# Outer tap columns of the offset sums moved by four transfers; the ninth sampling piece of a strip with 48 columns

## The chip, the core and the metric

One core of a Trainium2 chip runs the whole program in one launch. The metric is the device time in microseconds. TensorE (PE) multiplies, VectorE (DVE), ScalarE (ACT) and GpSimd (POOL) work element by element, SyncE (SP) issues transfers; ScalarE's queue can issue transfers as well.

## What is computed

Two metaformer layers on x of shape (4, 128, 128, 128). The change touches the first block alone, a deformable 3x3 convolution on the normalised input:

```python
def _L0_conv_ref(x, w_off, w_conv):              # x is _ln_c(x)
    offset = conv3x3(x, w_off, padding=1)        # 18 channels: (dy, dx) of 9 taps
    dy, dx = offset.reshape(B, 9, 2, H, W)[:, :, 0], ...[:, :, 1]
    py, px = base_y + dy, base_x + dx
    sampled = bilinear_gather(x, py, px)         # zero outside the image
    return einsum("bckhw,ock->bohw", sampled, w_conv)
x = x + _L0_conv_ref(_ln_c(x), w_off, w_conv)
```

A mixture of experts, a convolution by Fourier transform and a second mixture of experts follow. They are the same in both kernels.

## The kernel before

The first stage (`phase_a`) works in strips of four image rows; 4 images of 32 strips make 128 (the last of an image has six centre rows). `order_a` writes one list of steps for all engines: strip s has its time slots t0 to t0 + 11 (18 for the last of an image), `put(slot, step, ...)` puts a step into a slot, and each engine goes through the list and does the steps that are its own, in that order. Several strips are in the pipeline at once: in slot group s the letters are F = s + 4 (load, transpose, statistics, norm), Z = s + 2 (offset sums), N = s + 1 (weights of the samples), s itself (sampling), and s - 2 (output).

For one strip, in the order of the data:

- `turn` (L350, PE): four transposes of the input into a bank; `stats` (L496, L499, DVE): mean and variance; `scale` (L562 to L568, POOL): their power; `norm` (L437, ACT); `norm_out` (L446, ACT's queue): the normalised strip goes to DRAM (`xtp`).
- `conv` (L361, PE): 162 columns for each of four rows: the 18 offset channels for three tap rows and three tap columns, not yet summed; `y_out` (L464, ACT): scaled copies into the ring `a_yr`.
- `zsum` (L589, L595, POOL): the sum over the tap rows, into `zz`, with image x on the partitions. What is missing is the sum over the three tap columns kx, where kx = 0 and 2 belong to the neighbouring partition.
- `shift` (L374, PE): two matmuls with a shifted unit matrix do that move for kx = 0 and kx = 2, into a PSUM area `OF` (72 columns); `offs` (L517, DVE) adds kx = 1 and writes `on`, the offsets; `offs_out` (L450, ACT's queue) stores them.
- `place` (L623) and `hats` (L607, L610), POOL: distance of each offset from eight positions in x and in y; `bend` (L473, ACT) and `clip` (L528, DVE); `reach` (L522, L523, DVE): largest and smallest offset.
- `prod` (L536 on DVE, L576 on POOL): the products, 9 taps of 64 weights for each image row; `turn_s` (L545, DVE): their transposes into `tt`.
- `window` (L658, SP): 16 transfers of 36 KB from `xtp` to `win` for each strip. They wait for the store of the normalised strip. `x1_out` (L676) and `load` (L643) are 256 KB each on the same queue.
- `sample` (L405, PE): nine pieces of 36 positions in x of both halves, in three thirds h = 0, 1, 2. Each matmul uses 32 rows of the array, four stand side by side; fp32 makes two halves (instructions) of each, so 144 in all. Thirds 0 and 2 use banks 0 to 3, third 1 banks 4 to 7, where `turn` and `conv` write too. `evict` (L482 on ACT, L509 on DVE) copies each third into `a_sr`.
- `out` (L423, PE): nine matmuls with 512 columns, one for each tap; `residual` (L551, DVE) adds the input.

TensorE waits in this stage at the first third (transposed weights, windows), at the second third for `norm`, `stats`, `y_out` and `residual`, and at the third third for the emptying of the first.

## Time and profile before

| | us |
|---|---|
| median of three runs | 3873.46 (3870.35 to 3874.3) |
| the profiled execution | 3877.71 |
| its span, first to last instruction | 3875.7 |
| TensorE busy | 3679.2 |
| VectorE busy | 2944.7 |
| ScalarE busy | 1570.9 |
| GpSimd busy | 1474.4 |
| mean granted clock of TensorE | 0.956 |

The profile is of one execution. Its times are us from the first instruction, and a line Lnnn is one of the kernel before. A busy share is an average over stages; the stage of the change is the first half of the span. A row of the timeline merges neighbours of one line: start, length, engine, line, what it writes and reads, and how many instructions; brackets tell the idle time of the engine before it and who ended it.

### The profile page before, as it was taken

What the parts mean: (1) busy time and instruction counts of PE and PEld (TensorE: products, weight loads), DVE (VectorE), ACT (ScalarE), POOL (GpSimd) and SP (SyncE); (2) the same over time, 40 slices, a digit from 0 to 9 for tenths busy, and PEclk for the clock granted to TensorE, in tenths of its full rate; (3) what the DMA queues carried; (4) which work ended last, traced back from release to release, by engine and by line L of the source; (5) the groups of instructions that cost most, each with busy time, mean ns of one, the idle gap of its engine ahead of it and who ended that gap; (6) DMA issues with size and microseconds to landing.
All of it is one profiled execution on the core that took longest, in us unless ns stands there. A gap on an engine that the chain in (4) does not pass through costs nothing. (4 is left out here: it accounts for less than half of the span.)

```text
span 3875.7 us, 89814 instructions
## 1 busy us (share of the span) xinstructions
PE 3679.2 (95%) x31511; PEld 2470.7 (64%) x31511; DVE 2944.7 (76%) x9687; ACT 1570.9 (41%) x4565; POOL 1474.4 (38%) x2661
## 2 busy tenths in 40 slices
PE   6999999999999999999979999999999999996667
PEld 5777777777777777777745666666666666654444
DVE  4666666666666666666648999999999999996633
ACT  3444444444444444444411444434343443434224
POOL 4444444444454444444412333333333333333210
PEclk7999999999999999999979999999999999997755
DMA  5655555555555555555527777777777777884789
GB/s 109 108 95 108 100 95 97 96 108 104 91 99 95 108 103 94 96 97 97 88 81 265 270 275 274 272 268 273 277 271 275 267 276 273 285 303 158 268 312 393
DMA packets 611250, 709.81 MB, mean 183 GB/s; under 512 B 62208, under 2 KB 493824, under 8 KB 594416
## 3 DMA queue, kind: packets, MB, share of 16 engines
q1 hardware_dynamic: 505328, 630.10, 58.3%
q10 hardware_dynamic: 104448, 71.85, 6.0%
q8 instruction: 253, 4.15, 0.5%
q14 instruction: 197, 1.61, 0.2%
q0 software_dynamic: 1024, 2.10, 0.2%
HBM read 521.26 MB, written 181.50 MB: 181 GB/s over the span
## 5 line engine op out<-in xcount | busy, mean ns | idle before, releaser
L423 PE MATMUL a_sb<-a_sr,wcv 128*128 128x512 f32 (+3 forms) x2820 | 1052.2, 515 | 0.8 <-DVE a_xo L551 0.8
L405 PEld LDWEIGHTS a_sb<-a_tt,a_win 32*128 32x128 f32 x19008 | 647.0, 186 | 116.3 <-issue 115.5
L423 PEld LDWEIGHTS a_sb<-a_sr,wcv 128*128 128x128 f32 x2820 | 493.1, 190 | 333.9 <-issue 289.1
L405 PE MATMUL a_sb<-a_tt,a_win 32*128 32x144 f32 x19008 | 679.8, 295 | 17.5 <-ACT a_yr L464 11.0
L1171 DVE TENSOR_TENSOR b_P<-b_P,b_x 128x1024 f32<-128x1024 f32 x512 | 620.1, 1212 | 0.0
L509 DVE COPY a_sr<-a_sb 128x432 f32<-128x432 f32 (+14 forms) x1172 | 419.6, 413 | 204.1 <-PE a_sb L405 204.0
L482 ACT COPY a_sr<-a_sb 128x432 f32<-128x432 f32 (+14 forms) x1172 | 362.9, 389 | 356.4 <-PE a_sb L405 356.4
L1074 PE MATMUL b_z<-b_P,b_ew 128*128 128x512 f32 x1024 | 463.4, 596 | 0.0
L1077 PE MATMUL b_z<-b_P,b_ew 128*128 128x512 f32 x1024 | 460.3, 592 | 0.0
L1300 POOL TENSOR_TENSOR b_ss<-b_st 128x12 f32<-128x12 f32 (+2 forms) x139 | 29.9, 215 | 1050.6 <-DVE b_pp L1245 963.5
L545 DVE STREAM_TRANSPOSE a_tt<-a_sx 128x576 f32<-128x576 f32 x520 | 398.7, 768 | 14.2 <-POOL a_sx L576 5.4
L576 POOL TENSOR_TENSOR a_sx<-a_hh 128x576 f32<-128x576 f32 x260 | 307.5, 1183 | 126.7 <-DVE a_tt L545 123.3
L551 DVE TENSOR_TENSOR a_xo<-a_sb,a_xin 128x512 f32<-128x512 f32 x128 | 88.4, 691 | 345.3 <-PE a_sb L423 345.3
L1077 PEld LDWEIGHTS b_z<-b_P,b_ew 128*128 128x128 f32 x1024 | 194.7, 190 | 194.0 <-issue 187.9
L1074 PEld LDWEIGHTS b_z<-b_P,b_ew 128*128 128x128 f32 x1024 | 189.2, 195 | 185.2 <-issue 185.2
L1316 POOL TENSOR_TENSOR b_rs<-b_ss,mhalf 128x12 f32<-128x12 f32 (+2 forms) x139 | 302.0, 2172 | 11.1 <-POOL b_ss L1312 0.4
L437 ACT ACTIVATE a_tn<-a_sb,a_rs 128x128 f32<-128x128 f32 x512 | 192.4, 456 | 216.8 <-POOL a_rs L568 216.8
L473 ACT ACTIVATE a_hh<-a_hh 128x576 f32<-128x576 f32 (+1 forms) x128 | 88.3, 690 | 462.8 <-POOL a_hh L610 462.8
L1144 ACT ACTIVATE c_tn<-c_x,b_rs 128x128 f32<-128x128 f32 x512 | 163.7, 390 | 242.1 <-POOL b_rs L1316 242.1
L464 ACT ACTIVATE a_yr<-a_sb,zero,a_rs 128x162 f32<-128x162 f32 (+2 forms) x594 | 226.5, 467 | 57.0 <-ACT a_tn L437 57.0
L623 POOL COPY a_oc<-a_on 128x72 f32<-128x72 f32 x112 | 29.0, 259 | 548.7 <-DVE a_on L517 548.7
L361 PEld LDWEIGHTS a_sb<-wof,a_xin 128*128 128x128 f32 x1024 | 170.7, 195 | 85.3 <-issue 58.1
(186 smaller groups left out, 5374.3 us busy)
## 6 DMA issues: line engine op xcount, KB each, us to landing
b_P<-pd SPq DMA_DIRECT2D x128, 2048.0 KB, 7.8
a_win<-xtp SPq DMA_DIRECT2D x2144, 36.0 KB
a_xin<-in_x SPq DMA_DIRECT2D x128, 256.0 KB, 6.0
xtp<-a_tn ACTq DMA_DIRECT2D x128, 256.0 KB, 2.3
x1d<-a_xo SPq DMA_DIRECT2D x128, 256.0 KB, 5.7
b_x<-x1d SPq DMA_DIRECT2D x128, 256.0 KB, 7.7
x2d<-b_xa SPq DMA_DIRECT2D x128, 256.0 KB, 3.5
pw<-x3d SPq DMA_DIRECT2D x128, 256.0 KB, 6.6
```

The source lines that it names most:

```text
L405: t = e.matmul(d[:, 0:3 * m_, :, NU_ * i:NU_ * i + NU_], win[32 * q:32 * q + 32, half_of(Q, j) % NWH, NWIN // 3 * h + i, :], m, start=(j = ...
L423: t = e.matmul(ob[:, r:r + m, :], k["wcv"][:, 3 * (2 - kr) + kx, :], rows[:, :, t_, :], start=(t_ == 0 and r == 0), stop=(t_ == 8))
L437: a = e.activation(tn[:, G % NTN, r, :], TK[:, r, :], ACT.Identity, bias=rs[:, G % 2, r:r + 1], scale=rs[:, G % 2, 4 + r:5 + r])
L464: a = e.activation(yr[:, d:d + 216 * m].rearrange("p (k f) -> p k f", f=216)[:, :, 0:54], YB[r // 2][:, r % 2, 54 * kr:54 * (kr + m)].rear ...
L482: a = e.copy(d, v)
L509: a = e.tensor_copy(d, v)
L545: e.transpose(tt[:, Q % NTP, 0:2304].rearrange("p (j a t x) -> p a t j x", j=2, a=4, t=9)[:, n - quad(Q)[0]], sx[:, n % NST, :, :].rearran ...
L576: e.tensor_tensor(sx[:, n % NST, :, 0:NI * NJ].rearrange("p t (j i) -> p t j i", j=NJ), hh[:, G % 2, i, :, None, 0:NI].to_broadcast([128, ...
L1074: e.matmul(ZE[u][:, :, :], ew[:, x, :], P[:, G % NPB, :, x, :], start=(x == 0), stop=False)
L1077: e.matmul(ZE[u][:, :, :], ew[:, x, :], P[:, G % NPB, :, x, :], start=False, stop=False)
L1171: t = e.tensor_tensor(v, v, x1[:, G % NX1, r, None, :].to_broadcast([128, 8, 128]), ALU.mult)
L1316: e.tensor_tensor(rs[:, u, c], ss[:, u, 2, c], k["mhalf"][:, c], ALU.pow).then_inc(scaled, 1)
```

## The change

The two shift matmuls go, with their constant and their PSUM area. `shift` is now a step of ScalarE: four transfers inside SBUF, 112 and 15 partitions for each of kx = 0 and kx = 2, from `zz` (now laid out with kx outermost) to a new tile `zs`, one partition up or down. `offs` waits for all four and makes two additions. The ninth piece of the sampling leaves out the columns that no copy reads: 12 x 2 x 2 = 48 instead of 144. The slots move: `zsum` two earlier, `shift` two earlier, `offs` one later, `place`, `hats`, `offs_out`, `bend`, `reach` and `clip` one to three later and partly in another order, `y_out` one later, `scale` behind both `conv` steps, the products and their transposes two later.

```diff
@@ order_a
-                t = t0 + gap * i - 3
+                t = t0 + gap * i - 1
...
-            put(t0 + 4, "shift", Z)
-            put(t0 + 4, "offs", Z)
...
-            put(t0 + 6, "scale", F)
             put(t0 + 5, "conv", F, 0)
             put(t0 + 6, "conv", F, 1)
+            put(t0 + 6, "scale", F)
...
-            put(t0 + 8, "y_out", F, 0)
-            put(t0 + 9, "y_out", F, 1)
+            put(t0 + 9, "y_out", F, 0)
+            put(t0 + 10, "y_out", F, 1)
...
-            put(t0 + 1, "zsum", Z)
-            put(t0 + 5, "offs_out", Z)
-            put(t0 + 5, "place", Z)
-            put(t0 + 5, "hats", Z)
-            put(t0 + 6, "bend", Z)
-            put(t0 + 7, "reach", Z)
-            put(t0 + 7, "clip", Z)
+            put(t0 - 1, "zsum", Z)
+            put(t0 + 2, "shift", Z)
+            put(t0 + 5, "offs", Z)
+            put(t0 + 7, "place", Z)
+            put(t0 + 7, "hats", Z)
+            put(t0 + 7, "offs_out", Z)
+            put(t0 + 8, "bend", Z)
+            put(t0 + 8, "reach", Z)
+            put(t0 + 10, "clip", Z)
@@ tensor
                 w.wait_ge(y_ready, 4 * (G - 1) + 2 * h + 2)
-                if h:
-
-                    w.wait_ge(on_ready, shifts)
...
-            elif o[0] == "shift":
-                G = o[1]
-                bank_free()
-                w.wait_ge(z_step, z_count[G])
-
-                w.wait_ge(on_ready, G)
-                w.wait_ge(y_ready, 2 * convs)
-                shifts += 1
-
-                for kx in (0, 2):
-                    t = e.matmul(OF[:, :, :], k["shift"][:, kx, :], zz[:, G % 2, :, kx, :], start=(kx == 0),
-                                 stop=(kx == 2))
-                t.then_inc(shifted, 1)
...
-                        w.wait_ge(on_ready, shifts)
...
-                                m = bass.AP(m.tensor, m.offset, [list(m.ap[0]), [96, 3 * m_], [31, 3], [1, NU_]])
+                                t0, nx = (1, 2) if 3 * h + i == NWIN - 1 else (0, NU_)
+                                m = bass.AP(m.tensor, m.offset + 31 * t0,
+                                            [list(m.ap[0]), [96, 3 * m_], [31, 3 - t0], [1, nx]])
@@ scalar
+            elif o[0] == "shift":
+                G = o[1]
+                w.wait_ge(z_step, z_count[G])
+                w.wait_ge(filled, 1)
+                w.wait_ge(on_ready, G - 1)
+                for p, n in ((0, 112), (112, 15)):
+                    e.dma_start(zs[p + 1:p + n + 1, G % 2, 0, :, :], zz[p:p + n, G % 2, 0, :, :]
+                                ).then_inc(shifted[G % 2], 16)
+                    e.dma_start(zs[p:p + n, G % 2, 1, :, :], zz[p + 1:p + n + 1, G % 2, 2, :, :]
+                                ).then_inc(shifted[G % 2], 16)
@@ vector
-                w.wait_ge(shifted, G + 1)
+                w.wait_ge(shifted[G % 2], 64 * (G // 2 + 1))
+                w.wait_ge(z_step, z_count[G])
...
-                e.tensor_tensor(on[:, G % 2, :, :], OF[:, :, :], zz[:, G % 2, :, 1, :], ALU.add).then_inc(on_ready, 1)
+                e.tensor_tensor(on[:, G % 2, :, :], zs[:, G % 2, 0, :, :], zz[:, G % 2, 1, :, :], ALU.add
+                                ).then_inc(on_half, 1)
+                w.wait_ge(on_half, G + 1)
+                e.tensor_tensor(on[:, G % 2, :, :], on[:, G % 2, :, :], zs[:, G % 2, 1, :, :], ALU.add
+                                ).then_inc(on_ready, 1)
```

TensorE, from the second third of one sampling on, in a strip in the middle of an image, before:

```order
L405 MATMUL a_sb<-a_tt,a_win 128x36x4 [waits a_y_ready,a_x1_ready,a_mv_ready,a_normed]
L405 MATMUL a_sb<-a_tt,a_win 128x36x4 x23
L405 MATMUL a_sb<-a_tt,a_win 128x36x4 [waits a_taken_dve,a_taken_act]
L405 MATMUL a_sb<-a_tt,a_win 128x36x4 x23
L374 MATMUL a_sb<-a_zz,shift 128x72 [waits a_z_step,a_taken_dve,a_taken_act]
L374 MATMUL a_sb<-a_zz,shift 128x72
L350 MATMUL a_sb<-ident,a_xin 128x128 [waits a_x_in8]
L350 MATMUL a_sb<-ident,a_xin 128x128 x3
L423 MATMUL a_sb<-a_sr,wcv 128x512
```

And in the changed kernel, whose lines have other numbers (L390 is the sampling, L408 the output):

```order
L390 MATMUL a_sb<-a_tt,a_win 128x36x4 [waits a_y_ready,a_x1_ready,a_mv_ready,a_normed]
L390 MATMUL a_sb<-a_tt,a_win 128x36x4 x23
L390 MATMUL a_sb<-a_tt,a_win 128x36x4 [waits a_taken_dve,a_taken_act]
L390 MATMUL a_sb<-a_tt,a_win 128x36x4 x15
L390 MATMUL a_sb<-a_tt,a_win 128x12x2x2 x8
L350 MATMUL a_sb<-ident,a_xin 128x128 [waits a_x_in4,a_taken_dve,a_taken_act]
L350 MATMUL a_sb<-ident,a_xin 128x128 x3
L408 MATMUL a_sb<-a_sr,wcv 128x512
```

The wait for the emptying of the second third (a_taken) is now the transposes'.

ScalarE, from the emptying of the second third on, before (L450 and L446 are the stores of offsets and of the normalised strip, a_hh the bend, a_yr the y rows):

```order
L482 COPY a_sr<-a_sb 128x4x3x3x12 [waits a_sampled]
L482 COPY a_sr<-a_sb 128x4x3x3x12
L482 COPY a_sr<-a_sb 128x4x3x2x8 [waits a_sampled]
L482 COPY a_sr<-a_sb 128x4x3x2x9
L482 COPY a_sr<-a_sb 128x4x3x2x10
L450 DMA offd<-a_on 128x72 [waits a_on_ready]
L473 ACTIVATE a_hh<-a_hh 128x576 [waits a_hats_ready]
L437 ACTIVATE a_tn<-a_sb,a_rs 128x128 [waits a_tn_out2,a_rs_step]
L437 ACTIVATE a_tn<-a_sb,a_rs 128x128 x3
L446 DMA xtp<-a_tn 128x4x128 [waits a_normed]
L464 ACTIVATE a_yr<-a_sb,zero,a_rs 128x3x54 [waits a_convolved]
```

And in the changed kernel, from behind the second third's copies on:

```order
L460 DMA a_zs<-a_zz 112x72 [waits a_z_step]
L462 DMA a_zs<-a_zz 112x72
L460 DMA a_zs<-a_zz 15x72
L462 DMA a_zs<-a_zz 15x72
L477 COPY a_sr<-a_sb 128x4x3x2x8 [waits a_sampled]
L477 COPY a_sr<-a_sb 128x4x3x2x9
L477 COPY a_sr<-a_sb 128x4x3x2x10
L422 ACTIVATE a_tn<-a_sb,a_rs 128x128 [waits a_tn_out2,a_rs_step]
L422 ACTIVATE a_tn<-a_sb,a_rs 128x128 x3
L435 DMA offd<-a_on 128x72 [waits a_on_ready]
L431 DMA xtp<-a_tn 128x4x128 [waits a_normed]
L468 ACTIVATE a_hh<-a_hh 128x576 [waits a_hats_ready]
```

The transfers stand ahead of the last third's copies, the store of the normalised strip behind that of the offsets, and the y rows follow the bend, the last row here.

## Rows read from the trace of the kernel before

**Rows 1.** The page: span, and busy time, share of the span, instructions.

```profile
span 3875.7 us, 89814 instructions
PE 3679.2 (95%) x31511; PEld 2470.7 (64%) x31511; DVE 2944.7 (76%) x9687; ACT 1570.9 (41%) x4565; POOL 1474.4 (38%) x2661
```

**Rows 2.** Busy time by stage: stretch, its length, engines, clock, DMA share, GB/s.

```profile
0.00:1940.00 1940.00, 1897.94 (x23362) 1377.99 (x23362) 1299.33 (x3577) 863.41 (x2373) 929.15 (x1500) 0.99 0.55 99
```

**Rows 3.** Timeline of TensorE, one strip and the starts of the next two.

```profile
404.44 5.09 PE L405 MATMUL a_sb<-a_tt,a_win 32*128 32x144 f32 x144
409.45 0.67 PE L374 MATMUL a_sb<-a_zz,shift 128*128 128x72 f32 x4
409.95 0.60 PE L350 MATMUL a_sb<-ident,a_xin 128*128 128x128 f32 x4
...
419.31 1.88 PE L405 MATMUL a_sb<-a_tt,a_win 32*128 32x144 f32 x48
...
434.19 2.02 PE L405 MATMUL a_sb<-a_tt,a_win 32*128 32x144 f32 x52
```

**Rows 4.** The line that stores the offsets: its 128 issues and their landing.

```profile
L450 ACTq DMA_DIRECT2D offd<-a_on x128: 357/357/391, 25.5 to 1934.8; - x128
...
DMA to landing us min/median/max: 2.8/5.5/8.3
```

**Rows 5.** Timeline of ScalarE in the same strip.

```profile
408.00 0.97 ACT L482 COPY a_sr<-a_sb 128x432 f32<-128x432 f32 x2 [0.66 <-PE a_sb L405]
...
412.19 0.36 ACTq L450 DMA_DIRECT2D offd<-a_on  x1
413.94 0.68 ACT L473 ACTIVATE a_hh<-a_hh 128x576 f32<-128x576 f32 x1 [3.50 <-POOL a_hh L610]
416.28 1.50 ACT L437 ACTIVATE a_tn<-a_sb,a_rs 128x128 f32<-128x128 f32 x4 [1.66 <-POOL a_rs L568]
...
418.23 1.62 ACT L464 ACTIVATE a_yr<-a_sb,zero,a_rs 128x162 f32<-128x162 f32 x4 [0.45 <-ACT a_tn L437]
```

**Rows 6.** Timelines of ScalarE and of TensorE at the end of an image.

```profile
494.36 1.86 ACT L464 ACTIVATE a_yr<-a_sb,zero,a_rs 128x54 f32<-128x54 f32 x5 [0.44 <-ACT a_tn L437]
...
496.47 3.50 PE L405 MATMUL a_sb<-a_tt,a_win 32*128 32x144 f32 x96 [0.77 <-ACT a_yr L464]
```

**Rows 7.** Groups by line and shape, 0 to 2050 us: busy us, mean ns.

```profile
L405 PE MATMUL a_sb<-a_tt,a_win 32*128 32x144 f32 x18432 | 662.8, 296 | 17.5 <-ACT a_yr L464 11.0 <-DVE a_sr L509 2.8 <-issue 1.9
...
L374 PE MATMUL a_sb<-a_zz,shift 128*128 128x72 f32 x512 | 86.0, 291 | 9.5 <-ACT a_yr L464 5.4 <-POOL a_zz L595 4.1
```

**Rows 8.** Timeline of TensorE: a sampling of two rows, 72 columns a piece.

```profile
524.64 4.26 PE L405 MATMUL a_sb<-a_tt,a_win 32*128 32x72 f32 x144
```

**Rows 9.** The line that stores the normalised strip: landing.

```profile
DMA to landing us min/median/max: 2.3/2.3/8.6
```

**Rows 10.** Timeline of SyncE's queue in the same strip.

```profile
405.29 5.55 SPq L658 DMA_DIRECT2D a_win<-xtp  x16
410.89 0.36 SPq L676 DMA_DIRECT2D x1d<-a_xo  x1
411.30 0.43 SPq L643 DMA_DIRECT2D a_xin<-in_x  x1
```

**Rows 11.** Timeline of VectorE in the same strip.

```profile
408.00 1.12 DVE L509 COPY a_sr<-a_sb 128x432 f32<-128x432 f32 x2 [0.49 <-PE a_sb L405]
...
411.96 0.19 DVE L517 TENSOR_TENSOR a_on<-a_sb,a_zz 128x72 f32<-128x72 f32 x1
...
412.88 0.35 DVE L499 BATCH_NORM_AGGREGATE a_mv<-a_st 128x2 f32<-128x6 f32 x4
...
414.65 0.46 DVE L528 TENSOR_SCALAR a_hh<-a_hh 128x576 f32<-128x576 f32 x1 [0.52 <-ACT a_hh L473]
```

**Rows 12.** Timeline of GpSimd in the same strip.

```profile
412.22 0.24 POOL L623 COPY a_oc<-a_on 128x72 f32<-128x72 f32 x1 [5.04 <-DVE a_on L517]
...
413.21 0.70 POOL L610 TENSOR_TENSOR a_hh<-a_oc,cy 128x288 f32<-128x288 f32 x1
413.99 0.23 POOL L562 TENSOR_SCALAR a_rs<-a_mv 128x4 f32<-128x4 f32 x1
...
416.05 0.19 POOL L568 TENSOR_SCALAR a_rs<-a_rs 128x4 f32<-128x4 f32 x1
```

More of the change, by code:

```diff
@@ L74, in _ @@
             e.dma_start(k["ident"][:, :], ins["ident"][:, :]).then_inc(loaded, 16)
-            e.dma_start(k["shift"][:, :, :], ins["shift"][:, :, :]).then_inc(loaded, 16)
             e.dma_start(k["wcv"][:, :, :], ins["wcv"][:, :, :]).then_inc(loaded, 16)
@@ L78, in _ @@
             e.dma_start(k["cy"][:, :, :], ins["cy"][:, :, :]).then_inc(loaded, 16)
-            e.wait_ge(loaded, 80)
+            e.wait_ge(loaded, 64)
             e.wait_ge(w_in, 16)
@@ L250, in phase_a @@
     yr = S("a_yr", [128, NYR * 162 + 216])
-    zz = S("a_zz", [128, 2, 4, 3, 18])
+    zz = S("a_zz", [128, 2, 3, 4, 18])
+    zs = S("a_zs", [128, 2, 2, 4, 18])
     on = S("a_on", [128, 2, 4, 18])
@@ L271, in sem @@
         return sems[-1]
-    turned, convolved, shifted, sampled, conv_out = (
-        sem(n) for n in ("turned", "convolved", "shifted", "sampled", "conv_out"))
+    turned, convolved, sampled, conv_out = (
+        sem(n) for n in ("turned", "convolved", "sampled", "conv_out"))
+    shifted = [sem(f"shifted{i}") for i in range(2)]
     normed, y_ready, bent, taken_act = (sem(n) for n in ("normed", "y_ready", "bent", "taken_act"))
     taken_dve = sem("taken_dve")
+    on_half = sem("on_half")
     filled, bn_done, mv_ready, on_ready, reached, clipped, weighed_dve, turned_s, x1_ready = (
@@ L333, in tensor @@
         w = Once(e)
-        convs = shifts = outs = taken = 0
+        convs = outs = taken = 0
         def bank_free():
@@ L488, in vector @@
         e.memset(sx[:, :, :, :], 0.0)
+        e.memset(zs[:, :, :, :, :], 0.0)
         e.memset(tt[:, :, 2304:2306], 0.0).then_inc(filled, 1)
@@ L1789, in program @@
             SA = lambda name, shape, dt=F32: ca.enter_context(nc.sbuf_tensor(name, shape, dt))
-            k |= {"zero": SA("zero", [128, 640]), "wof": SA("wof", [128, 162]), "shift": SA("shift", [128, 3, 128]), "wcv": SA("wcv", [128, 9, 128]),
+            k |= {"zero": SA("zero", [128, 640]), "wof": SA("wof", [128, 162]), "wcv": SA("wcv", [128, 9, 128]),
                   "cx": SA("cx", [128, 9, NI]), "cy": SA("cy", [128, 14, NJ])}
@@ L1813, in constants @@
     ident = np.eye(128, dtype=np.float32)
-    shift = np.zeros((128, 3, 128), np.float32)
-    for kx in range(3):
-        x = np.arange(max(0, 1 - kx), min(128, 129 - kx))
-        shift[x + kx - 1, kx, x] = 1.0
     x, t, i = np.arange(128)[:, None, None], np.arange(9)[None, :, None], np.arange(NI)[None, None, :]
@@ L1837, in constants @@
     rev = np.ascontiguousarray(ident[:, (128 - np.arange(128)) % 128])
-    return {"io": io, "pick": pick, "rev": rev, "ident": ident, "shift": shift, "cx": np.ascontiguousarray(cx), "cy": np.ascontiguousarray(cy), "base": base, "far": far}
+    return {"io": io, "pick": pick, "rev": rev, "ident": ident, "cx": np.ascontiguousarray(cx), "cy": np.ascontiguousarray(cy), "base": base, "far": far}
 OUTN = ["out"]
```

8 lines of the change are left out of this document (3 added, 5 removed).

## The prediction

> **What bounds the kernel now.** I read the page first, then the busy time by stage, then the timeline of one strip on each engine. The page says TensorE is busy 95% of the span [rows 1]. The edit touches only the first stage, and there TensorE works 1897.9 of 1940 us at 0.99 of its clock [rows 2]. The timeline says what a strip is: sampling (144 matmul halves, 5.01 us up to the next step), the two shift matmuls (409.45 to 409.95, 0.50 us), four transposes, then the offset and the output matmuls, until the next sampling starts 14.87 or 14.88 us after this one [rows 3]. There are 128 strips [rows 4], and 128 x 14.88 = 1905 us is the stage. A microsecond taken from TensorE's work in each strip is worth 128 us, as long as nothing else ends last. What ends next to last is the second third of the sampling, which waits for the y rows of ScalarE: the rows end at 419.85 and that third starts at about 419.31 + 48 x 33.5 ns = 420.92 [rows 3, 5], so 0.8 us are spare once the 0.25 us is taken off that TensorE needs to start behind them (rows end at 496.22, TensorE starts at 496.47 [rows 6]).
>
> **TensorE's work.** The shift matmuls go: 0.50 us a strip, start to start [rows 3]. They are four halves of 291 ns mean, but pipelined [rows 7], so the start-to-start value is the one to take. Their waits (for the offset sum, before the second offset matmul) only cost idle time of the weight loader, not of the array.
>
> The ninth piece has 16 of the 144 halves of a sampling, with 48 columns for 144. Halves of 144 columns follow each other at (5.09 - 0.30)/143 = 33.5 ns, halves of 72 columns at (4.26 - 0.27)/143 = 27.9 ns [rows 3, 7, 8]: half the columns give back only 5.6 ns, so something other than columns is nearly as long. Lower bound: 16 x 5.6 ns = 0.09 us. Upper bound, if the time went by columns alone: 5.01 x 1/9 x 2/3 = 0.37 us. I take 0.12, next to the row of 72 columns, and a little for the shorter last matmul, behind which the transposes wait. The Trainium skill (TensorE: Matmul & The Clock Gate, LDWEIGHTS) says that a weight load takes P/1.2 ns for P columns whatever the rows, so 107 ns for each of the four row groups; four times 27.9 ns is 112 ns, and the trace agrees. By that rule the ninth piece would give 4 x (134 - 107) ns = 0.11 us.
>
> Together 0.62 us: a strip of TensorE's work is 14.26 us instead of 14.88, and the sum is 128 x 0.62 = 79 us.
>
> **What comes in its place.** The sums now come from four transfers on ScalarE's queue, issued after ScalarE has emptied the second third. It ends that at 408.97, 4.53 us after the sampling started [rows 5]. An issue takes 0.36 us and about 0.04 between, so the four start at 4.55, 4.95, 5.35 and 5.75. The last third is emptied 1.2 us later than now; only the next sampling needs those banks, 8 us later, so that is free.
>
> VectorE then waits for all four. Call L the time from the last issue to its landing; the sum starts at X = 5.75 + L. The nearest row is the transfer that writes the same 128 x 288 bytes to DRAM from the same queue: 2.8 us at best, 5.5 median, 8.3 at worst [rows 4]. The next one, 256 KB from the same queue when the window loads wait, lands in 2.3 us [rows 9]. Why 5.5: it is issued 6.9 us after the first window load of the strip, behind 16 of them and both 256 KB transfers (405.29, 410.89, 411.30; 412.19) [rows 5, 10]. The last shift transfer stands in much the same crowd: window loads would start near -0.3 in the new strip and end their issue near 5.3. It has only one of the two large transfers before it, but three of its own. I take 5.5, and keep 2.8 and 6.5 as ends.
>
> From X, by the durations of the same steps today: both additions and the hand-over 0.45 (0.26 now, plus 0.19 for the second addition), place and hats 1.69, bend 0.71, y rows 1.78 (they stand behind bend now), the start of TensorE 0.25: 4.88 us [rows 5, 6, 11, 12]. The second third of the next sampling stands at 14.26 + 1.61. If it waits s, the next transfers are issued s later too: 5.75 + s + L + 4.88 = 14.26 + s + 1.61 + s, that is s = L - 5.24. **Up to a landing of 5.24 us the wait is hidden; beyond it each 0.1 us costs 13 us in all; at 5.86 us the whole gain is gone.** With L = 5.5, s = 0.26 and a strip is 14.52 us.
>
> **The other moves.** On VectorE a transpose now stands before the emptying of the last third, and the statistics come directly after that: 4.67, 5.4, 6.3, then means at 7.5 after the start, where they end at 8.79 today. GpSimd does the scale before the hats: four steps in 2.25 us (413.99 to 416.24), so 9.75. Norm on ScalarE ends near 11.3 instead of 13.34 [rows 5, 11, 12]. The store of the normalised strip stands behind the store of the offsets, so behind X + 0.45, which at X = 11.25 is no later than today. The clip, the products and the transposes behind X give: clip X + 3.3, product X + 4.1, residual and transpose X + 5.5, the emptying of the first third X + 6.6; TensorE needs that at 14.26 + 3.2 + s, which is met or short by some tenths in the same cases, so it is no price of its own. The second half of the strip's transposes ends at X + 2.0 and is needed at 14.26. The second addition (0.19 us), the wider clearing at the start and the other order of elements in the column sums lie on engines that are busy under 70% of this stage [rows 2]: nothing. One load less in the set-up is beside longer ones: nothing. The four image ends, where the pipeline already stalls by about a microsecond [rows 6], I leave as they are.
>
> **The sum.** 128 x (14.88 - 14.52) = 46 us off 3877.7 us, the profiled execution: 3831.6. That execution is 4.2 us over the median of the runs, so the forecast is **3827 us**.
>
> **Rivals.**
> TensorE stays the bound (L under 5.24). For it: the best landing is 2.8, the target is not DRAM, and one of the two 256 KB transfers is behind it and not ahead. Then the full 79 us: 3794 us, down to 3785 if the ninth piece gives twice what I take. The Trainium skill (DMA: Bandwidth & Descriptors, Anatomy of one DMA) puts a small transfer at some 2.0 us, most of it the receipt of the target memory; by it X would be 7.8 and this rival would be the result. The 5.5 us row speaks against it in this crowd.
>
> The landing takes the bound and gives the gain back (L over 5.86). Four transfers put 16 rows on each of the DMA engines where the offset store puts 8; they queue behind the window loads. And there is a loop: the normalised strip's store now waits for the sum, the window loads wait for that store, and the next shift transfers queue behind the window loads, so a late landing makes the next crowd later. With L = 6.2, s = 0.96, a strip is 15.22 us: 128 x 0.34 = 44 us slower, 3917 us.
>
> Nothing measurable: L between 5.8 and 5.95, 3866 to 3881 us.
>
> The change doesn't do what it says: the same data must be summed, so the only doubt is whether TensorE's 0.50 us really closes up. If the transposes start no sooner because they wait for the emptying of the second third (VectorE ends it at 409.12, 4.68 us in; the sampling ends at 4.9) the gain is smaller. That is 0.2 us of room, little, but enough [rows 3, 11].
>
> **How the numbers follow.** Forecast (a landing-bound wait in part of the strips) 0.35, with a range of its own from 3803 to 3862; TensorE-bound 0.35; no difference 0.08; slower 0.22. Differences under 0.2% (8 us) can't be told from none here. Faster 0.70, same 0.08, slower 0.22. The range leaves out the far end of the slower case and what lies below 3785: 3785 to 3900.
>
> **What would show it.** Sampling to sampling: 14.26, 14.5 or over 14.9 us. Right: no L374, transposes within 0.1 us of the sampling's end, ninth piece some 0.1 us shorter. The forecast: idle time of TensorE before the second third, ended by the y rows, 0.2 to 0.3 us a strip, and VectorE idle 2 to 3 us before the first addition, ended by the transfer. No such idle time on TensorE: the first rival. Over 0.6 us: the second. Wrong altogether: waits for the transposed weights at a sampling's start, or normalised strips stored later than today.

## The result, and the profile after

The changed kernel takes 4008.89 us, the median of four runs (4003.53 to 4013.9), beside 3872.43 us for the kernel before on the same chip: a ratio of 1.0352, with a 95% interval of 1.0334 to 1.037. The forecast was 3827 us and the range 3785 to 3900. The change costs 136.5 us. The time lies outside the range, and the side is the one that had a chance of 0.22.

The page of the changed kernel, the parts that answer to [rows 1]: span, busy time, and two groups of its fifth part.

```profile
span 4009.7 us, 89430 instructions
...
PE 3647.7 (91%) x30999; PEld 2431.1 (61%) x30999; DVE 2928.5 (73%) x9816; ACT 1548.5 (39%) x4565; POOL 1551.5 (39%) x2661
...
L390 PE MATMUL a_sb<-a_tt,a_win 32*128 32x144 f32 (+1 forms) x19008 | 704.4, 297 | 180.7 <-DVE a_xo L552 112.3
...
L514 DVE TENSOR_TENSOR a_on<-a_zs,a_zz 128x72 f32<-128x72 f32 x128 | 29.9, 234 | 563.7 <-DMA a_zs<-a_zz 563.7
```

TensorE is busy for 31.5 us less in a span that is 134 us longer. The sampling, which in [rows 7] had sat idle for 17.5 us in all, now does so for 180.7 us, most of it for the residual of VectorE. VectorE itself waits 563.7 us for the new transfers, in every one of the 128 strips: 4.4 us a strip.

The two halves of the span, after (the columns of [rows 2]):

```profile
0.00:2075.00 2075.00, 1867.93 (x22846) 1337.63 (x22847) 1280.25 (x3701) 840.11 (x2372) 1002.23 (x1498) 0.98 0.53 97
2075.00:4009.00 1934.00, 1779.82 (x8155) 1093.44 (x8153) 1648.21 (x6116) 708.36 (x2193) 549.28 (x1164) 0.92 0.76 267
```

What lies behind the first stage takes 1934 us, beside 1936 before (3875.7 less 1940). The loss is all in the first stage. The granted clock, 0.98 beside 0.99 there, is not where it comes from: in this stretch of 500 us it is 1.00 in both kernels, before and then after, and TensorE's busy time is 498 us of it in one and 460 in the other.

```profile
600.00:1100.00 500.00, 498.25 (x6154) 359.48 (x6153) 339.50 (x934) 224.34 (x620) 242.15 (x396) 1.00 0.55 99
```

```profile
600.00:1100.00 500.00, 459.66 (x5660) 326.75 (x5658) 315.55 (x913) 205.20 (x584) 245.91 (x370) 1.00 0.53 97
```

One strip on TensorE and the sampling behind it, answering to [rows 3]:

```profile
1002.33 4.95 PE L390 MATMUL a_sb<-a_tt,a_win 32*128 32x144 f32 x144
1007.21 0.66 PE L350 MATMUL a_sb<-ident,a_xin 128*128 128x128 f32 x4
...
1017.32 1.88 PE L390 MATMUL a_sb<-a_tt,a_win 32*128 32x144 f32 x48 [0.58 <-issue]
1020.37 3.41 PE L390 MATMUL a_sb<-a_tt,a_win 32*128 32x144 f32 x96 [1.17 <-DVE a_xo L552]
...
1033.12 1.09 PE L390 MATMUL a_sb<-a_tt,a_win 32*128 32x144 f32 x24
```

The transposes now start 4.88 us after the sampling (5.51 in [rows 3]): the 0.62 us that the prediction counted are there. But the next sampling starts 14.99 us after this one and the one behind it 15.80 us later. The next one is 0.58 us late at its first third, for the transposed weights, and stops again for 1.17 us before its second third.

The same strip on ScalarE, answering to [rows 5]: a copy of the second third, the four transfers, the last third's copies, the norm, the two stores, the bend and the y rows.

```profile
1005.88 0.54 ACT L477 COPY a_sr<-a_sb 128x432 f32<-128x432 f32 x1 [0.66 <-PE a_sb L390]
...
1005.88 0.60 ACTq L460 DMA_DIRECT2D a_zs<-a_zz  x1
1006.52 0.63 ACTq L462 DMA_DIRECT2D a_zs<-a_zz  x1
1007.18 1.47 ACTq L460 DMA_DIRECT2D a_zs<-a_zz  x1
1008.67 0.86 ACTq L462 DMA_DIRECT2D a_zs<-a_zz  x1
1009.57 0.83 ACT L477 COPY a_sr<-a_sb 128x192 f32<-128x192 f32 x3 [2.72 <-issue]
1012.05 1.51 ACT L422 ACTIVATE a_tn<-a_sb,a_rs 128x128 f32<-128x128 f32 x4 [1.65 <-POOL a_rs L569]
1015.90 0.37 ACTq L435 DMA_DIRECT2D offd<-a_on  x1
1016.30 0.44 ACTq L431 DMA_DIRECT2D xtp<-a_tn  x1
1017.65 0.68 ACT L468 ACTIVATE a_hh<-a_hh 128x576 f32<-128x576 f32 x1 [4.09 <-POOL a_hh L611]
1018.24 1.80 ACT L449 ACTIVATE a_yr<-a_sb,zero,a_rs 128x54 f32<-128x54 f32 x5
```

And on VectorE (the two additions are L514 and L517) and SyncE's queue:

```profile
1015.36 0.23 DVE L514 TENSOR_TENSOR a_on<-a_zs,a_zz 128x72 f32<-128x72 f32 x1 [5.12 <-DMA a_zs<-a_zz]
...
1015.78 1.43 DVE L546 STREAM_TRANSPOSE a_tt<-a_sx 128x576 f32<-128x576 f32 x2
...
1019.53 0.68 DVE L552 TENSOR_TENSOR a_xo<-a_sb,a_xin 128x512 f32<-128x512 f32 x1
```

```profile
1001.86 6.63 SPq L659 DMA_DIRECT2D a_win<-xtp  x16
...
1018.69 6.83 SPq L659 DMA_DIRECT2D a_win<-xtp  x16
```

Read in order: the last transfer is issued at 1008.67, the sum starts at 1015.36, which is 6.7 us later (the prediction took 5.5). Everything behind the sum is then in a row: the transposes of VectorE end at 1017.21 and TensorE starts its sampling at 1017.32; the y rows end at 1020.04, the residual at 1020.21, and TensorE starts the second third at 1020.37, 5.01 us after the sum. The normalised strip has been ready since 1013.56, but its store stands behind the store of the offsets on ScalarE's queue and is issued at 1016.30. The window loads, which need it, start at 1018.69. That is the loop that the prediction named.

Over the strips of this execution I took the start of each sampling, the start of its transfers and the last increment of their semaphore from the records; the medians are a strip of 15.86 us, the last issue 7.20 us after the sampling's start, and a landing 6.65 us behind that issue (5.57 to 6.86 for the middle half of the strips). "L" below is always this time from the start of the last issue to the last landing, median over the strips, and X the start of the sum after the sampling's start. The four transfers of a strip count up one semaphore, and the profile deals its increments out in order of time. So L is measured, but the landing that a row gives for one of the four lines is not that of a single transfer.

### The profile page after: what moved, and what is told of

Its sections match the earlier page's. It is cut to its first block and busy times, and to the rows that moved or that the text cites. A ratio compares the mean times of both kernels' runs of the same rounds, so it can differ in the third digit from the quotient of the medians.

```text
span 4009.7 us, 89430 instructions
## 1 busy us (share of the span) xinstructions
PE 3647.7 (91%) x30999; PEld 2431.1 (61%) x30999; DVE 2928.5 (73%) x9816; ACT 1548.5 (39%) x4565; POOL 1551.5 (39%) x2661
## 5 line engine op out<-in xcount | busy, mean ns | idle before, releaser
L408 PE MATMUL a_sb<-a_sr,wcv 128*128 128x512 f32 (+3 forms) x2820 | 1052.3, 515 | 0.8 <-DVE a_xo L552 0.8
L390 PE MATMUL a_sb<-a_tt,a_win 32*128 32x144 f32 (+1 forms) x19008 | 704.4, 297 | 180.7 <-DVE a_xo L552 112.3
L390 PEld LDWEIGHTS a_sb<-a_tt,a_win 32*128 32x128 f32 x19008 | 665.6, 188 | 303.6 <-issue 300.3
L408 PEld LDWEIGHTS a_sb<-a_sr,wcv 128*128 128x128 f32 x2820 | 492.8, 190 | 334.0 <-issue 288.9
L577 POOL TENSOR_TENSOR a_sx<-a_hh 128x576 f32<-128x576 f32 x260 | 378.1, 1454 | 489.2 <-DVE a_tt L546 322.7
L505 DVE COPY a_sr<-a_sb 128x432 f32<-128x432 f32 (+14 forms) x1172 | 410.6, 403 | 75.7 <-PE a_sb L390 75.6
L514 DVE TENSOR_TENSOR a_on<-a_zs,a_zz 128x72 f32<-128x72 f32 x128 | 29.9, 234 | 563.7 <-DMA a_zs<-a_zz 563.7
L546 DVE STREAM_TRANSPOSE a_tt<-a_sx 128x576 f32<-128x576 f32 x520 | 386.4, 761 | 1.9 <-POOL a_sx L577 1.4
L537 DVE TENSOR_TENSOR a_sx<-a_hh 128x576 f32<-128x576 f32 x260 | 194.2, 747 | 4.3
```

The source lines that it names most:

```text
L390: t = e.matmul(d[:, 0:3 * m_, t0:3, NU_ * i:NU_ * i + nx], win[32 * q:32 * q + 32, half_of(Q, j) % NWH, NWIN // 3 * h + i, :], m, start=(j ...
L408: t = e.matmul(ob[:, r:r + m, :], k["wcv"][:, 3 * (2 - kr) + kx, :], rows[:, :, t_, :], start=(t_ == 0 and r == 0), stop=(t_ == 8))
L505: a = e.tensor_copy(d, v)
L537: e.tensor_tensor(sx[:, n % NST, :, 0:NI * NJ].rearrange("p t (j i) -> p t j i", j=NJ), hh[:, G % 2, i, :, None, 0:NI].to_broadcast([128, ...
L546: e.transpose(tt[:, Q % NTP, 0:2304].rearrange("p (j a t x) -> p a t j x", j=2, a=4, t=9)[:, n - quad(Q)[0]], sx[:, n % NST, :, :].rearran ...
L577: e.tensor_tensor(sx[:, n % NST, :, 0:NI * NJ].rearrange("p t (j i) -> p t j i", j=NJ), hh[:, G % 2, i, :, None, 0:NI].to_broadcast([128, ...
```

## Experiments

All of them are timed beside the kernel before. Line numbers are those of each kernel, so the same step can have another one.

### Without the transfers (e1_no_transfers)

```diff
@@ scalar, shift
-                for p, n in ((0, 112), (112, 15)):
-                    e.dma_start(zs[p + 1:p + n + 1, G % 2, 0, :, :], zz[p:p + n, G % 2, 0, :, :]
-                                ).then_inc(shifted[G % 2], 16)
-                    e.dma_start(zs[p:p + n, G % 2, 1, :, :], zz[p + 1:p + n + 1, G % 2, 2, :, :]
-                                ).then_inc(shifted[G % 2], 16)
@@ vector, offs
-                w.wait_ge(shifted[G % 2], 64 * (G // 2 + 1))
+                w.wait_ge(filled, 1)
```

(A `pass` stands in place of the transfers.) The kernel leaves the outer tap columns out of the offset sums.

> The changed kernel without the four transfers and without the wait for them: the tap columns kx = 0 and 2 are left out of the offset sums (zs stays zero). All slots and both additions stay. Theory landing (TensorE waits only because the sums come late): a strip takes TensorE's own work, 14.88 - 0.58 = 14.30 us, so 128 x 0.58 = 74 us under the kernel before, about 3798 us, and TensorE is never idle before the second third. Rival order (the moved slots cost by themselves): the time stays above 3872 us and TensorE still waits for the residual or the y rows.

Measured: 3793.85 us (3789.29 to 3795.7), ratio 0.9791 [0.9775, 0.9807]. A strip is 14.29 us. So the new order of steps, the second addition, the later y rows and the ninth piece cost TensorE nothing, and the whole of the 0.6 us would arrive if the sums were there in time. What the transfers themselves do to the kernel is 4009 − 3794 = 215 us.

### The ninth piece alone (e2_ninth_only)

```diff
@@ tensor, sample (in the kernel before)
-                                m = bass.AP(m.tensor, m.offset, [list(m.ap[0]), [96, 3 * m_], [31, 3], [1, NU_]])
+                                t0, nx = (1, 2) if 3 * h + i == NWIN - 1 else (0, NU_)
+                                m = bass.AP(m.tensor, m.offset + 31 * t0,
+                                            [list(m.ap[0]), [96, 3 * m_], [31, 3 - t0], [1, nx]])
...
-                                t = e.matmul(d[:, 0:3 * m_, :, NU_ * i:NU_ * i + NU_],
+                                t = e.matmul(d[:, 0:3 * m_, t0:3, NU_ * i:NU_ * i + nx],
```

> The kernel before with only the ninth piece cut from 144 to 48 columns. Prediction's term: 0.09 to 0.37 us a strip, taken as 0.12: 15 us less, about 3857 us. After's trace, whose sampling is 4.88 us instead of 5.01 us, says 0.13 us: 3856 us. If columns alone counted: 3825 us.

Measured: 3859.38 us (3858.0 to 3861.34), ratio 0.9957 [0.9943, 0.9971]. That is 16.6 us or 0.13 us a strip, where the prediction took 0.12 from the row of 72 columns [rows 8].

### The normalised strip's store first (e3_store_first)

```diff
@@ order_a
-            put(t0 + 7, "offs_out", Z)
+            put(t0 + 8, "offs_out", Z)
```

With this the store of the normalised strip no longer stands behind the sum, and the loop is cut.

> The changed kernel with the store of the normalised strip ahead of the store of the offsets on ScalarE's queue, nothing else. In after the store of the normalised strip waits some 2.3 us for the sums (norm ends at 1013.56, the store is issued at 1016.30). Theory loop (a late sum makes the next window loads late, and these make the next transfers late): the window loads start 2 us earlier against the strip, the transfers have fewer of them ahead, and the time falls by 60 us or more, to 3950 us or under. Theory crowd without a loop: the window loads only overlap the transfers differently, the last landing stays 5 to 7 us after its issue, and the time stays within 20 us of 4009 us.

Measured: 3950.13 us, ratio 1.0194 [1.0175, 1.0212]. The first theory had set 60 us or more for the loop, and this is just short of it; the other, within 20 us of 4009, is out. The place of the store is worth 4009 − 3950 = 59 us, and with the store out from behind the sum the kernel is still slower than before. What VectorE waits for between 100 and 1900 us of this kernel (us in total, times, longest):

```profile
DVE a_on L514 <- DMA a_zs<-a_zz: 430.3, 114, 8.6
```

The wait for the transfers stays in nearly every strip; it is 483.2 us in the changed kernel. L is 5.68 us here beside 6.65, X 12.62 beside 13.86, a strip 15.36 beside 15.86.

### The transfers issued but not waited for (e10_not_waited)

```diff
@@ scalar, shift
-                    e.dma_start(zs[p + 1:p + n + 1, G % 2, 0, :, :], zz[p:p + n, G % 2, 0, :, :]
+                    e.dma_start(zt[p + 1:p + n + 1, G % 2, 0, :, :], zz[p:p + n, G % 2, 0, :, :]
...
@@ vector, offs
-                w.wait_ge(shifted[G % 2], 64 * (G // 2 + 1))
+                w.wait_ge(filled, 1)
```

All four transfers go to a tile `zt` that nobody reads, so the sums lack the outer tap columns; `zsum` waits for the transfers two strips later.

> The changed kernel with all four transfers issued at the same place on ScalarE, into a tile that nothing reads, and no wait for them in the sums (the outer tap columns are left out of the sums). Theory landing (only the wait of the sums for the last landing costs time): 3794 us within 10, as without the transfers, though each still takes 0.6 to 0.9 us to issue and lands late. Theory issue (ScalarE held up for 2.5 to 4 us a strip moves the last third's copies and the norm past what TensorE can hide): 3830 us or more, with TensorE idle before the second third.

Measured: 3794.89 us (3792.7 to 3797.33), ratio 0.9791 [0.9775, 0.9807], the same as without any transfer. So neither the time that ScalarE spends on the issues nor what they take from the other transfers costs anything: it is the wait alone. This run is also the cleanest look at the landing, in a pipeline that stalls nowhere. Its issues in one strip, and the line of the second and fourth transfer with its landing (min/median/max over both of them):

```profile
1014.88 4.95 PE L391 MATMUL a_sb<-a_tt,a_win 32*128 32x144 f32 x144
...
1018.45 0.60 ACTq L461 DMA_DIRECT2D a_zt<-a_zz  x1
...
1020.63 0.86 ACTq L463 DMA_DIRECT2D a_zt<-a_zz  x1
```

```profile
L463 ACTq DMA_DIRECT2D a_zt<-a_zz x256: 604/857/2050, 24.6 to 1855.9; - x128
...
DMA to landing us min/median/max: 1.8/5.3/9.8
```

The last of the four starts 5.75 us after the sampling, to the hundredth where the prediction had it, and in the median of the strips 5.76. L is 6.13 us, with no loop and no stall in it. The sum, which waits for nothing, starts at X = 7.84.

### The transfers ahead of the window loads (e4_sync_queue)

```diff
@@ order_a
-            put(t0 + 2, "shift", Z)
+            put(t0 - 1, "shift", Z)
@@ scalar
-            elif o[0] == "shift":
...
@@ sync
+            elif o[0] == "shift":
...
```

The branch with the four transfers moves to SyncE's queue unchanged, one slot ahead of the sampling, where the window loads of the same slot stand behind it.

> The changed kernel with the four transfers on SyncE's queue, one sampling earlier in the order, directly ahead of the strip's window loads; all else as changed. Theory crowd (they land late because window loads stand before them on the DMA engines): they land about 2 us after the last issue, well before VectorE gets to the sum 7.2 us into the strip, TensorE's idle time goes, about 3800 us. Theory issue (a transfer inside SBUF is slow by itself): landing stays 5 us or more after the last issue, but begins earlier, 3850 us or more. If window loads, now 2.4 us later, become the bound, TensorE waits for them at a sampling's start: above 3872 us.

Measured: 3842.85 us (3840.93 to 3844.21), ratio 0.9916 [0.99, 0.9933]. The strip is 14.29 us. One strip of SyncE's queue with the sum on VectorE, and the landing of the second and fourth transfer:

```profile
1314.50 0.56 SPq L656 DMA_DIRECT2D a_zs<-a_zz  x1
...
1316.64 0.83 SPq L658 DMA_DIRECT2D a_zs<-a_zz  x1
1317.58 6.54 SPq L649 DMA_DIRECT2D a_win<-xtp  x16
1320.52 0.23 DVE L504 TENSOR_TENSOR a_on<-a_zs,a_zz 128x72 f32<-128x72 f32 x1
```

```profile
L658 SPq DMA_DIRECT2D a_zs<-a_zz x256: 557/821/1989, 24.4 to 1901.6; - x128
...
DMA to landing us min/median/max: 1.8/2.4/5.4
```

The same four transfers take just as long to issue, but this row has 2.4 us where e10 has 5.3, and the sum waits for nothing (X is 7.84, as in e10). What is lost against 3794 lies at the start and the ends of the images, where the window loads now stand behind transfers whose data come later: TensorE waits for windows in four places, 56.6 us in all. The first sampling of the program:

```profile
69.61 5.66 PE L390 MATMUL a_sb<-a_tt,a_win 32*128 32x144 f32 x113 [35.30 <-DMA a_win<-xtp]
```

It starts at 69.6 us, and at 38.65 without the transfers.

### Window loads ahead on the same queue (e5_windows_ahead)

```diff
@@ order_a, beside the move of e4
-            while windows < B * NHALF and (windows < NWH or last_quad(windows - NWH) < Q):
+            out.append(("sample", Q))
+            while windows < B * NHALF and last_quad(windows - NWH) <= Q:
                 out.append(("window", windows))
                 windows += 1
-            out.append(("sample", Q))
...
```

Besides the lines shown, the first four loads are also listed behind the first four stores of normalised strips.

> The four transfers on SyncE's queue as in e4_sync_queue, and each window load listed behind the sampling that frees its buffer instead of ahead of the next one, the first four behind the first four stores of normalised strips. In e4_sync_queue a strip is already 14.29 us, and TensorE waits 56.6 us for windows in four places, at the start and at the three image ends, where the loads stand behind transfers that wait for their sums. Theory crowd: nothing else is missing, so these 50 us go and the time is that of e1_no_transfers, 3794 us (within 10). Rival: the loads, now issued 5 us into a strip and 6 us long, meet the next strip's transfers or come too late for the sampling: 3843 us or more.

Measured: 4150.09 us, ratio 1.0712 [1.0695, 1.073], the worst of all, and not what I had expected. SyncE's queue and the sum in one strip:

```profile
1299.85 5.54 SPq L653 DMA_DIRECT2D a_win<-xtp  x16
...
1306.39 0.57 SPq L660 DMA_DIRECT2D a_zs<-a_zz  x1
...
1308.53 0.83 SPq L662 DMA_DIRECT2D a_zs<-a_zz  x1
1313.22 0.23 DVE L508 TENSOR_TENSOR a_on<-a_zs,a_zz 128x72 f32<-128x72 f32 x1 [5.36 <-DMA a_zs<-a_zz]
```

The window loads wait for the normalised strip's store, that store waits for the previous sum, and the transfers now wait for both: here the loop runs through one queue, the first issue comes 8 us after the sampling's start and X is 15. L is 4.4 us, less than in the changed kernel, so this loss is of the issue and not of the landing. In e4 the transfers stand ahead of the same loads; the other order of loads and transfers costs 307 us.

### Half of the window loads (e6_half_loads)

```diff
@@ sync, window
-                    for q in range(4):
+                    for q in (0, 1):
...
```

Besides the lines shown, the counts that TensorE waits for are halved, and the other half of the window buffers is set to zero.

> The changed kernel with half of the window loads left out (8 of the 16 transfers of 36 KB a strip; the other half of the window buffers holds zeros), the four shift transfers as changed. Theory crowd: the last of the four lands 3 to 4.5 us after its issue instead of 6.65, VectorE's wait shrinks by 2 us or more, and the time falls to 3800 to 3850 us. Theory issue (the 0.6 to 1.5 us that each issue takes and a landing that is slow by itself): the last landing stays over 6 us after its issue, the time within 30 us of 4009 us.

Measured, in two runs: 3810.9 us (3806.89 to 3814.91), ratio 0.984 [0.982, 0.9859]. The transfers are issued at the same place of the same queue as in the changed kernel; what else is in flight is halved, and its issue ends sooner. L falls from 6.65 to 2.63 us (6.13 in e10, where nothing stalls either), X is 8.6 and a strip 14.29. Landing of the second and fourth transfer:

```profile
DMA to landing us min/median/max: 1.8/2.7/6.4
```

So the late landing comes from the window loads, and a transfer inside SBUF isn't slow by itself.

### A shorter chain behind the sum (e7_chain)

```diff
@@ order_a
-            put(t0 + 9, "y_out", F, 0)
-            put(t0 + 10, "y_out", F, 1)
+            put(t0 + 8, "y_out", F, 0)
+            put(t0 + 8, "y_out", F, 1)
...
-            put(t0 + 12, "residual", s - 2)
+            put(t0 + 11, "residual", s - 2)
```

The y rows go ahead of the bend and the residual ahead of the product: the two steps that TensorE waits for at the second third.

> The changed kernel with the y rows ahead of the bend on ScalarE and the residual ahead of the product on VectorE. The sums come no earlier; what stands between them and TensorE's second third gets shorter: the y rows no longer depend on the sums except through two stores ahead of them, the residual ends at X + 4.0 instead of X + 4.85. Theory chain (TensorE waits there for X + 4.9): the wait of the second third shrinks by 0.8 us or more of about 1.2 to 1.5, the wait at the sampling's start (transposes at X + 1.85) stays: 3870 to 3930 us. Rival (something else late, as the window loads, sets the strip): within 20 us of 4009 us.

Measured: 4046.68 us, ratio 1.0438 [1.0419, 1.0457], slower than the changed kernel. Both expectations missed it: the first had 3870 to 3930 us, the rival no more than 20 us from 4009. Waits of TensorE between 100 and 1900 us, the changed kernel first, then this one:

```profile
PE a_sb L390 <- DVE a_xo L552: 100.3, 93, 1.9
PE a_sb L390 <- issue: 37.0, 43, 2.3
```

```profile
PE a_sb L390 <- DVE a_sr L505: 109.3, 103, 1.2
PE a_sb L390 <- DVE a_xo L552: 39.4, 53, 1.3
```

The wait for the residual shrinks, and a new one of the same size comes up a third later: the emptying of the first third (L505), which had been pushed behind on VectorE. So more than one chain behind the sum is that long, and this reordering doesn't pay; others were not run. What did pay in every run is an earlier sum.

### Without the two small transfers (e8_two_transfers)

```diff
@@ scalar, shift
-                for p, n in ((0, 112), (112, 15)):
+                for p, n in ((0, 112),):
@@ vector, offs
-                w.wait_ge(shifted[G % 2], 64 * (G // 2 + 1))
+                w.wait_ge(shifted[G % 2], 32 * (G // 2 + 1))
```

The kernel leaves the last 15 partitions of both outer tap columns out of the sums.

> The changed kernel without the two transfers of 15 rows (the last 15 partitions of both outer tap columns are left out of the sums). In after the four issues start 5.00, 5.63, 6.30 and 7.20 us into a strip and the last ends at 8.07. Theory issue: the sum comes at least 1.6 us earlier and a strip gets 1.6 us shorter, TensorE's own work is nearly the bound: 3800 to 3830 us. Theory crowd: the 112-row transfers stand behind the same window loads and land at nearly the same time as the small ones, so the gain is under half of that: 3900 to 3980 us.

Measured, in two runs: 3836.3 us (3833.79 to 3838.81), ratio 0.9905 [0.9885, 0.9925]. Both expectations missed it, and the miss is the useful part. The landing is as late as with four, L 6.45 us; but the second and last issue starts at 4.15 us, not at 5.76, so X is 10.8, and that is just early enough: a strip is 14.34 us. Landing of the second transfer of the pair, and what TensorE waits for between 100 and 1900 us:

```profile
DMA to landing us min/median/max: 1.8/6.3/9.3
```

```profile
PE a_sb L390 <- DVE a_xo L552: 18.1, 24, 1.8
```

The prediction puts the X up to which a late sum is hidden at 5.75 + 5.24 = 11.0. This run fits that from below: at 10.8 TensorE waits 18 us for the residual, where the changed kernel waits 100 us for it in the same stretch. But 10.8 is a median, and four strips in ten lie over 11. From one second third to the next it takes 14.4 us in the mean where X is under 10.5, 14.65 where it is 11 to 12 and 15.3 where it is 12 to 13. The late strips pay and the early ones give nothing back, so the kernel stays 42 us over e1. The two small transfers cost 173 us here. X is 3.0 us later with them: 1.6 us are their issue and 0.2 us the landing. The rest fits what a late sum does to the next strip's issues, 7.20 instead of 5.76 after the sampling's start.

### Window loads ahead at the ends alone (e9_ends_ahead)

```diff
@@ order_a, beside the move of e4
+            b, i = divmod(windows, NHALF)
+            if (windows < B * NHALF and last_quad(windows - NWH) <= Q
+                    and ("norm_out", b * GI + min(i, GI - 1)) in out):
+                out.append(("window", windows))
+                windows += 1
...
```

Besides the lines shown, the first four loads are listed behind the first four stores, as in e5.

> The four transfers on SyncE's queue as in e4_sync_queue; at the start and the image ends, where the data of the window loads are there long before, the loads are listed ahead of the transfers: the first four behind the first four stores of normalised strips, and at an image end each right behind the sampling that frees its buffer. In e4_sync_queue a strip is 14.29 us and TensorE waits 56.6 us for windows in four places. Theory crowd: those waits go and nothing comes in their place: 3790 to 3800 us, the time of e1_no_transfers. Rival: the first strip of each image has its transfers behind 16 loads and waits there instead; four times 5 us or more stay: 3810 to 3840 us.

Measured: 3843.02 us (3840.34 to 3844.39), ratio 0.9912 [0.9895, 0.9929], no different from e4's 3842.85. The first sampling comes at 56.03 instead of 69.61 us, and the time is lost again further on, at the ends of the images, in strips of 16.5 to 19.5 us. Which of the waits costs it there, and whether another order on this one queue would do without them, was not separated.

### Both queues (e11_two_queues)

```diff
@@ order_a
-            put(t0 + 2, "shift", Z)
+            if Z % GI < 3:
+                put(t0 + 2, "shift_a", Z)
+            else:
+                put(t0 - 1, "shift", Z)
...
```

The first three strips of an image (`shift_a`) go by ScalarE's queue, as in the changed kernel, the others by SyncE's, as in e4.

> As e4_sync_queue (the four transfers on SyncE's queue ahead of the strip's window loads), but for the first three strips of each image the four are issued by ScalarE at the place of the changed kernel, so that at the start and the image ends no window load stands behind a transfer that waits for its sums. Theory crowd: the 56.6 us of window waits go, the twelve strips with a late landing cost 1 to 2 us each instead: 3800 to 3815 us. Rival (the pipeline's turn at an image end is bound by something else, as it was with the loads ahead, 3843 us): 3835 us or more.

Measured: 3824.43 us (3811.93 to 3825.98), ratio 0.9873 [0.9856, 0.9889], which beats both kernels. Waits of VectorE for the transfers between 100 and 1900 us, and the first sampling:

```profile
DVE a_on L517 <- DMA a_zs<-a_zz: 35.5, 14, 6.5
```

```profile
47.27 6.69 PE L393 MATMUL a_sb<-a_tt,a_win 32*128 32x144 f32 x144 [7.54 <-DVE a_tt L549]
```

The profiled execution is the fastest of the four, 12.5 us under their median, so what follows covers the smaller part of the 31 us between this kernel's median and e1's. It has a span of 3810.1 us, 22.7 more than that of the kernel without transfers: 9 of them are this first sampling (38.65 there), 8 more have come by the last sampling of the stage, and the rest lies behind it.

## Why the prediction was wrong

**TensorE's work: right.** 0.62 us a strip, 14.26 us; measured 14.29 in e1, e4, e10 and e11. The ninth piece gave 0.13 for 0.12 (e2). What the prediction says of the trace's agreement on weight loads holds for their spacing, 112 ns; the records of the single loads of L405 before the change last 183 ns in the median.

**The issues: two errors that cancel.** The first starts 3.56 us after the sampling and not at 4.55, since it doesn't wait for the copies ahead of it to end (copy and issue are both at 1005.88 in the strip above). Each takes 0.60 to 0.86 us and more instead of the 0.36 us of [rows 4], which is the issue of a store to DRAM. The last starts at 5.76 (e10), forecast 5.75.

**The chain behind the sum: nearly right.** 4.88 us forecast; 5.01 in the strip above. In the medians the second third starts 3.05 us after a sampling's start, and 15.86 + 3.05 − 13.86 is 5.05 us.

**The landing: the term that failed.** I took 5.5 us, the median of one row, the offset store in [rows 4], and argued that the crowd would be "much the same". Measured where nothing stalls it is 6.13 (e10). By the prediction's own rule, s = L − 5.24, that is s = 0.89, a strip of 15.15 us and 128 x 0.27 = 35 us slower: 3908 us. The break-even at 5.86 us was 0.36 us from the value taken, and in [rows 4] the landing spreads from 2.8 to 8.3. At 13 us for each tenth, the sign of the forecast hung on a third of a microsecond of a row that was not of this operation. That row also told of one transfer, and the sum waits for the latest of four. How much that makes isn't shown: with two transfers L is 6.45 us (e8), no less than with four. What is shown is that the landing is set by the window loads (e6: 2.63 us behind half of them). The argument of the first rival, a short landing by itself, holds as far as it goes, with 1.8 us at best; it didn't come true because of those loads. The 2.0 us that this rival takes from the Trainium skill (DMA: Bandwidth & Descriptors, Anatomy of one DMA) is given there for transfers that GpSimd issues, and these are ScalarE's.

**"No later than today": failed with it.** The store of the normalised strip was said to be harmless at X = 11.25. At X = 13.9 it is not: the windows start later, against the transfers of the next strip, and L grows to 6.65. The rival had named this loop and given it no price of its own; e3 gives it, 59 us. With L = 6.65 and the chain of 4.88 as forecast, the rule gives s = 1.41 and a strip of 15.67 us; 15.86 were measured. With the chain of 5.05 it gives 15.84, but that is no test, because the 5.05 was worked out from the 15.86.

**"No price of its own" for the steps behind the sum: half wrong.** They do end together, as forecast (transposes at X + 1.85, forecast 2.0; residual at X + 4.85, forecast 5.5). But TensorE met two of them in the same strip, for 0.58 us before the first third and 1.17 before the second, and in e7 another before the last.

**Start and ends, left as they are: 9 us.** The first sampling before, and after the change:

```profile
39.31 2.33 PE L405 MATMUL a_sb<-a_tt,a_win 32*128 32x144 f32 x48 [1.81 <-DMA a_win<-xtp]
```

```profile
48.61 7.56 PE L390 MATMUL a_sb<-a_tt,a_win 32*128 32x144 f32 x144 [7.55 <-DVE a_tt L546]
```

**The sum of it.** 128 x (15.86 − 14.89) = 124 us, by the median strips of both kernels, and 9 us at the start: 133 of the 136.5 us.

What each term has of it is read from means, which add up where medians don't. A strip, counted from second third to second third, has three parts: from the second third's start to the last issue, the landing, and the chain from the sum to the next second third. The means are over the strips between 100 and 1900 us that take 13.5 to 20 us.

| us, means | second third to last issue | landing | chain | strip |
|---|---|---|---|---|
| forecast | 4.14 | 5.50 | 4.88 | 14.52 |
| changed kernel | 4.43 | 6.30 | 5.21 | 15.98 |
| e3, store first | 4.44 | 5.70 | 5.27 | 15.42 |

In the changed kernel the landing has 0.8 us of the 1.46 and is the largest miss; the other two have 0.3 each. In e3 they have more than the landing, and the rule with its L of 5.68 gives 14.87 us, half a microsecond too little. Part of that is the spread, which the prediction's one value for L leaves out. In a strip whose sum is early the chain has slack (5.5 us and more at X under 12, where its median is 5.0 in both kernels), and the late strips get nothing of it. How the rest divides isn't shown.

So the second rival came true, with its mechanism and its sign, but at L = 6.65 where it stood at 6.2, and at three times its cost of 44 us. The size was missed by the rival too. The chances were the second error: what decided between it and the forecast was L over or under 5.86, and 0.22 was too little for a value whose only row gave 5.5 as its median and 8.3 as its end. The bounds of L that the prediction kept, 2.8 to 6.5, gave 3794 to 128 x 0.64 = 82 us slower, about 3955; the range stopped at 3900. (One slip in the sums: at L = 5.95 the rule gives 12 us slower, 3885 and not 3881.)

What stays open is what inside the DMA engines holds the transfers up. The packets' records narrow it. The four transfers of a strip are 254 packets of 288 bytes, and one takes 20 ns in the median in the changed kernel. In its median strip 72 of them start over 2 us behind the last issue, 16 over 3 us and the last one at 5.7; in e6 none starts over 2 us behind it. So a part of the packets starts late, and the sum waits for the last; the packets themselves are not slow. Whether they wait for one engine's backlog, for memory or for their turn between two queues, no run tells.

## What to carry to other kernels

Price a small transfer by what is in flight when it is issued, and by the latest part that the engine waits for; if the sign of the result turns within the spread of that row, give both sides and not that row's median. A spread costs by itself where early arrivals are not given back. A transfer on a path that sets the end belongs ahead of the bulk loads (e4, e11), and its own issue times (here 0.6 to 0.9 us each, four in a row) are part of the path. Before putting a wait ahead of anything on a queue, follow what stands behind it around to the start: here a store behind the sum led through the window loads back to the sum.

## What the runs showed of the hardware

A transfer of 32 or 4 KB inside SBUF landed in 1.8 us at best. The last of a strip's four landed, in the median, 6.13 us behind its issue when issued behind 16 window loads of 36 KB (e10), and 2.63 us behind eight of them (e6). The rows of the second and fourth give 5.3 and 2.7 us for these, and 2.4 us where the four go ahead of the 16 loads (e4). The offset store, which had landed in 5.5 us [rows 4], lands in 1.6 us after the change. It is now issued before the window loads (1015.90 and 1018.69 above) and not behind them (412.19 and 405.29, [rows 5, 10]). Its line in the changed kernel:

```profile
L435 ACTq DMA_DIRECT2D offd<-a_on x128: 365/366/399, 35.2 to 2073.9; - x128
...
DMA to landing us min/median/max: 1.5/1.6/9.4
```

It was the same transfer, from the same queue, in other company. The Trainium skill (DMA: Bandwidth & Descriptors, Queues, rings and completion order) says that each DMA engine takes turns between the queues it has work for, a packet at a time. By that alone a short transfer on ScalarE's queue would not stand behind the whole of a long backlog on SyncE's, only behind its turns. The trace neither confirms nor refutes it: 182 of the 254 packets have started within 2 us of the last issue, yet the last lands at 6.65, and at 2.63 with half the loads.

The issue of a transfer from SBUF to SBUF took 0.53 to 2.4 us, on ScalarE (median 0.75 and 0.86 for the two lines) and on SyncE (0.74 and 0.82) alike, where the store to DRAM took 0.36 to 0.40. The four of a strip kept ScalarE's queue for 3.1 us, and where nobody waited for their landing even that cost nothing (e10).
